# Row sums on TensorE by four f32 matmuls of 32 columns, in a two-layer graph network kernel

## The chip, the cores and the metric

One core of a Trainium2 chip. The metric is the device time of one execution in microseconds (us), the median of several runs.

## The reference

Two graph layers over a dense adjacency matrix of 8192 x 8192 and features of 8192 x 128, all f32, each with a residual and a layer norm:

```python
def _L0_gnn_ref(X, adj, W, b):
    adj_hat = adj + jnp.eye(adj.shape[0], dtype=adj.dtype)
    d_inv_sqrt = 1.0 / jnp.sqrt(jnp.sum(adj_hat, axis=1))
    adj_norm = adj_hat * d_inv_sqrt[:, None] * d_inv_sqrt[None, :]
    out = adj_norm @ (X @ W) + b
    return jax.nn.relu(out)

def _L1_gnn_ref(x, adj, weight, self_weight):
    support = x @ weight
    output = support + adj @ support
    output = output + x @ self_weight
    output = jax.nn.relu(output)
    return pair_norm(output)          # mean of columns taken off, one common scale

x = _layernorm(x + _L0_gnn_ref(x, adj, L0_gnn_W, L0_gnn_b), axis=-1)
x = _layernorm(x + _L1_gnn_ref(x, adj, L1_gnn_weight, L1_gnn_self_weight), axis=-1)
```

The first layer can multiply a column block of adj only when the row sums (degrees) of the same rows are known, since they scale the features.

## The kernel before

adj is cut into 8 x 8 blocks of 1024 x 1024, and each block into four chunks of 1 MiB (128 partitions x 2048). A chunk has two slices of 128 x 1024. The host lays adj out twice, transposed (adjT) and plain (adjN).

**Products.** f32 products are made of f32r parts. For a slice ScalarE writes the rounded value into one of four buffers hi (L558), VectorE writes the rest, raw - hi, as raw_low over the raw chunk itself (L726: `twin` at L321 gives one place in SBUF two names, f32 and f32r), and TensorE does six matmuls of 128 stationary x 512 moving columns (L1043, L1045, L1049) into a pair of PSUM banks. In the trace the low part is raw_low, s_low, zr_low or o_low, after the place in which the chunk lies. Semaphores carry this: `hi_ready`, `slice_split`, `slice_multiplied`. ScalarE may be four slices ahead of TensorE (DEEP = 4).

**Degrees.** In the first phase blocks on and above the diagonal are needed for row sums before their product. Row sums right of the diagonal come from adjN chunks of kind "sum" on ScalarE (L564) or VectorE (L732), the diagonal's from VectorE additions into colsum (chunks "keep", L742, L746). Those of blocks below the diagonal are taken by TensorE while it has them for the product: chunks with `summed`, 112 of them. For each of their slices, `add_sums` multiplies hi and low with a window of `pick`, 128 x 128 and zero but for one column of ones, into pC and pD (L1025). The window's place chooses the PSUM partition in which the sums of this row block collect. `close_sums` (L1061, f32) adds colsum when a row block is complete, ScalarE copies pC and pD into t1 and t2 (L573), and `turn_degree` (L1071) picks partition k out of them with one column of ident, as a column per 128 rows. Then come square root, reciprocal and the scaled features of this row block.

**Order.** One list, `chunks`, sets the order on all engines. The first phase runs over 12 units (a row block's q quarters of 256 rows). In a unit the products of the previous rows stand mixed with the sum chunks of the next. Two more phases follow: both layers' products together, then what is left of the second layer's. SyncE issues the loads in the same order (L486 keep, L493 others), each into the buffer that has been free longest, and waits where that is still in use. The buffers of the first phase are raw0 to raw5 and five borrowed places: s34 and s56 throughout, z67 up to row block 5, z45 up to 3, z23 up to 1. TensorE, ScalarE, VectorE and SyncE each work through their own part strictly in this order.

Of the kernel before, what the change touches and what calls it, by code (L numbers as in the profile page):

```python
# [8 lines left out]
class Chunk:  # L9
# [7 lines left out]
    cached: bool = False  # L17
    act: bool = False
    summed: bool = False
    stage: int = -1  # L20
    tail: int = -1
    buf: str = ""
# [30 lines left out]
def graph_kernel(nc, x, xT, adjT, adjN, W0, b_rows, W1, Wself, out):  # L53
    f32 = mybir.dt.float32
# [5 lines left out]
    P = 128  # L60
# [12 lines left out]
    BG = BLK // P  # L73
    DEEP = 4
    PLACES = 4
    EPS_LN = 1e-5
    EPS_PN = 1e-6
    L0, L1 = 0, 1
# [107 lines left out]
    after_row0 = next(c for c in chunks if c.stage == 1)  # L186


    slices = act_sums = dve_sums = 0
    for chunk in chunks:  # L190
        if chunk.kind == "mul":
            chunk.base = slices
            slices += JB
            chunk.freed = ("multiplied", slices)
            visits[chunk.visit].end = slices
        elif chunk.kind == "sum" and chunk.act:
            act_sums += 1
            chunk.freed = ("act", act_sums)
        elif chunk.kind == "sum":
            dve_sums += 1  # L200
            chunk.freed = ("dve", dve_sums)
# [2 lines left out]

    BORROWED = {"s34": NB - 1, "s56": NB - 1, "z67": 5, "z45": 3, "z23": 1}
    LATE = ("z67", "z45", "z23")
    free_buffers = deque([(f"raw{r}", ()) for r in range(6)] + [(b, ()) for b in BORROWED])
    loads = defaultdict(int)
    phase1_last = {}
    late = False  # L210
    for chunk in chunks:
        if chunk.kind == "keep" or chunk.cached:
            continue
        phase = visits[chunk.visit].phase if chunk.kind == "mul" else 1
        if phase == 3 and not late:
            late = True
            free_buffers.extend((b, ("split", chunk.base)) for b in LATE)
        while phase < 3 and free_buffers[0][0] in BORROWED and (
                phase == 2 or units[chunk.stage][0] > BORROWED[free_buffers[0][0]]):
            free_buffers.popleft()  # L220
        chunk.buf, chunk.after = free_buffers.popleft()
        loads[chunk.buf] += 1
        chunk.load = loads[chunk.buf]
        free_buffers.append((chunk.buf, chunk.freed))
        if phase == 1:
            phase1_last[chunk.buf] = chunk.freed
# [84 lines left out]
    with ctx:  # L311
        def sb(name, shape, dt=f32):
            return ctx.enter_context(nc.sbuf_tensor(name, shape, dt))
# [4 lines left out]
        def sem(name):  # L318
            return ctx.enter_context(nc.semaphore(name))
# [18 lines left out]
        w1 = sb("w1", [P, P])  # L338
        wsum = sb("wsum", [P, P])
        ident = sb("ident", [P, P])  # L340
        rows = sb("rows", [P, P])
        pick = sb("pick", [P, P + NB - 1], f32r)
        d = sb("d", [P, N // P])
# [44 lines left out]
        ident_ready = sem("ident_ready")  # L388
        pick_zero = sem("pick_zero")
        setup = sem("setup")  # L390
        hi_ready = sem("hi_ready")
        slice_split = sem("slice_split")
        slice_multiplied = sem("slice_multiplied")
# [81 lines left out]
        def low_of(chunk, j):  # L475
            if chunk.cached:
                return o1_low[:, chunk.q * TILE + j * BLK:chunk.q * TILE + (j + 1) * BLK]
            return raw_low[chunk.buf][:, j * BLK:(j + 1) * BLK]

        @block.sync  # L480
# [216 lines left out]
        def _(dve):  # L697
# [15 lines left out]
            V.memset(pick[:, NB - 1:NB].bitcast(f32), 1.0).then_inc(setup, 1)  # L713
            dve.wait_ge(consts_in, 64)
            V.tensor_add(wsum[:, :], w1[:, :], t1[:, 0:P]).then_inc(setup, 1)

            def split_lo(chunk):
                for j in range(JB):
# [296 lines left out]
        def _(pe):  # L1015
            T = nc.tensor
            closed = [0]

            def add_sums(chunk, n):

                pe.wait_ge(sums_read, closed[0])
                to = pick[:, NB - 1 - chunk.row:NB - 1 - chunk.row + P]
                for h in range(H):
                    for mov in (hi[n % DEEP][:, :], low_of(chunk, n - chunk.base)):
                        last = T.matmul(sums[h][:, :], to, mov[:, h * HALF:(h + 1) * HALF],  # L1025
                                        start=False, stop=False, skip_group_check=True)
                return last

            def multiply(chunk):
                v = visits[chunk.visit]  # L1030
                for j in range(JB):
                    n = chunk.base + j
                    pe.wait_ge(slice_split, n + 1)
                    end = n == v.end - 1
                    for l, s in zip(chunk.layers, chunk.slots):
                        banks = acc[v.sets[l]]
                        opens = chunk.opens and j == 0
                        for by, count in v.waits[l] if opens else ():
                            pe.wait_ge(bank_free[by], count)
                        a, b = rhi[s][:, j * P:(j + 1) * P], rlo[s][:, j * P:(j + 1) * P]  # L1040
                        for h in range(H):
                            part = slice(h * HALF, (h + 1) * HALF)
                            T.matmul(banks[h][:, :], a, hi[n % DEEP][:, part], start=opens, stop=False,  # L1043
                                     skip_group_check=True)
                            T.matmul(banks[h][:, :], a, low_of(chunk, j)[:, part], start=False, stop=False,  # L1045
                                     skip_group_check=True)
                        for h in range(H):
                            part = slice(h * HALF, (h + 1) * HALF)
                            last = T.matmul(banks[h][:, :], b, hi[n % DEEP][:, part], start=False, stop=end,  # L1049
                                            skip_group_check=True)  # L1050
                        if end and chunk.layers == (L0, L1) and l == L0:
                            last.then_inc(l0_closed, 1)
                    if chunk.summed:
                        last = add_sums(chunk, n)
                    last.then_inc(slice_multiplied, 1)

            def close_sums(k):
                pe.wait_ge(col_step, (k + 1) * (JB * Q - 1))
                to = pick[:, NB - 1 - k:NB - 1 - k + P].bitcast(f32)
                for h in range(H):  # L1060
                    last = T.matmul(sums[h][:, :], to, colsum[:, h * HALF:(h + 1) * HALF],  # L1061
                                    start=(k == 0), stop=True, skip_group_check=True)
                last.then_inc(sums_closed, 1)
                closed[0] = k + 1

            def turn_degree(k):
                pe.wait_ge(sums_read, k + 1)
                if k > 0:
                    pe.wait_ge(z_ready, unit_of[k, 0])
                for g in range(BG):  # L1070
                    last = T.matmul(pA[:, g:g + 1], (t1, t2)[g // G][:, g % G * P:g % G * P + P], ident[:, k:k + 1],  # L1071
                                    start=True, stop=True)
                last.then_inc(deg_turned, 1)

# [52 lines left out]
            pe.wait_ge(consts_in, 64)  # L1127
            pe.wait_ge(setup, 2)
            pe.wait_ge(ident_ready, 1)
            close_sums(0)  # L1130
            turn_degree(0)
            first_product(0)
# [54 lines left out]
```

## Time and profile before

| | us |
|---|---|
| median of 3 runs | 1891.78 |
| lowest, highest | 1887.06, 1892.68 |
| profiled execution | 1891.55 |
| its span | 1889.8 |

The profile shows one execution. Engines: PE is TensorE's matmuls, PEld its weight loads, DVE is VectorE, ACT is ScalarE, SPq is the queue on which SyncE issues loads. A busy share is a mean over the span. Matmuls overlap in their pipeline, so two rows that start 0.23 us apart may each last 0.39 us; the distance of starts is what one costs. L12 is line 12 of the kernel.

### The profile page before, as it was taken

What the parts mean: (1) busy time and instruction counts of PE and PEld (TensorE: products, weight loads), DVE (VectorE), ACT (ScalarE), POOL (GpSimd) and SP (SyncE); (2) the same over time, 40 slices, a digit from 0 to 9 for tenths busy, and PEclk for the clock granted to TensorE, in tenths of its full rate; (3) what the DMA queues carried; (4) which work ended last, traced back from release to release, by engine and by line L of the source; (5) the groups of instructions that cost most, each with busy time, mean ns of one, the idle gap of its engine ahead of it and who ended that gap; (6) DMA issues with size and microseconds to landing.
All of it is one profiled execution on the core that took longest, in us unless ns stands there. A gap on an engine that the chain in (4) does not pass through costs nothing.

```text
span 1889.8 us, 20584 instructions
## 1 busy us (share of the span) xinstructions
PE 1752.6 (93%) x7682; PEld 1418.1 (75%) x7682; DVE 1488.8 (79%) x1985; ACT 1205.6 (64%) x1640; POOL 21.3 (1%) x42
## 2 busy tenths in 40 slices
PE   2879998987999999989999999999989999999993
PEld 1657886865887888767788888888868888877872
DVE  4889788767878789986777575575589999999997
ACT  4576685784757556654554554455468888888875
POOL 0000000000000000100000000000000000000001
PEclk7899999998999999999999999999999999999995
DMA  9999999899898686954544445555589999999943
GB/s 398 421 421 421 417 400 422 337 392 394 348 402 345 234 356 244 358 197 148 174 163 189 167 175 197 182 178 189 191 304 385 385 388 386 386 379 366 386 193 89
DMA packets 87459, 572.03 MB, mean 303 GB/s; under 512 B 8960, under 2 KB 17152, under 8 KB 19264
## 3 DMA queue, kind: packets, MB, share of 16 engines
q1 hardware_dynamic: 84928, 562.07, 75.8%
q0 software_dynamic: 2432, 8.65, 1.4%
q8 instruction: 60, 0.98, 0.2%
q14 instruction: 39, 0.32, 0.0%
HBM read 566.49 MB, written 4.19 MB: 302 GB/s over the span
## 4 chain that ended last, share of the span: by engine, by line
PE 74%; DVE 14%; DMA 6%; ACT 4%; issue 2%; SPq 0%; ACTq 0%; DVEq 0%
PE acc L1043 18%; PE acc L1045 18%; PE acc L1049 18%; DMA raw<-in_adjT 4%; PE pC L1025 4%; PE pD L1025 4%; DVE raw_low L726 4%; DMA s<-in_adjN 2%; ACT hi L558 2%; DVE o_low L726 1%; DVE s L732 1%; DVE zr_low L726 1%; DVE ux L805 1%; PE pA L1043 1%; PE pB L1045 1%
## 5 line engine op out<-in xcount | busy, mean ns | idle before, releaser
L1043 PE MATMUL acc<-hi,rhi 128*128 128x512 f32 x1792 | 726.3, 405 | 76.3 <-DVE raw_low L726 25.0
L726 DVE TENSOR_TENSOR raw_low<-raw,hi 128x1024 fp32r<-128x1024 f32 x576 | 684.3, 1220 | 84.4 <-ACT hi L558 79.8
L558 ACT ACTIVATE hi<-raw 128x1024 fp32r<-128x1024 f32 x576 | 593.7, 1055 | 195.3 <-DMA raw<-in_adjT 68.3
L1049 PE MATMUL acc<-hi,rlo 128*128 128x512 f32 x1792 | 559.9, 394 | 0.0
L1045 PE MATMUL acc<-raw_low,rhi 128*128 128x512 f32 x1348 | 530.7, 394 | 0.0
L1043 PEld LDWEIGHTS acc<-hi,rhi 128*128 128x128 f32 x1792 | 341.7, 191 | 173.4 <-DVE raw_low L726 35.0
L1049 PEld LDWEIGHTS acc<-hi,rlo 128*128 128x128 f32 x1792 | 341.2, 190 | 73.7
L1045 PEld LDWEIGHTS acc<-raw_low,rhi 128*128 128x128 f32 x1348 | 256.2, 190 | 54.9 <-issue 3.6
L726 DVE TENSOR_TENSOR zr_low<-zr,hi 128x1024 fp32r<-128x1024 f32 x148 | 177.6, 1221 | 30.4 <-ACT hi L558 27.9
L558 ACT ACTIVATE hi<-zr 128x1024 fp32r<-128x1024 f32 x148 | 155.2, 1059 | 58.4 <-PE pD L1025 24.0
L725 DVE TENSOR_TENSOR rlo<-zr,rhi 128x256 fp32r<-128x256 f32 x123 | 52.0, 423 | 177.5 <-ACT hi L558 177.5
L552 ACT ACTIVATE rhi<-zr 128x256 fp32r<-128x256 f32 x123 | 50.8, 413 | 191.7 <-PE acc L1049 190.3
L564 ACT ACTIVATE raw<-raw 128x1024 f32<-128x1024 f32 x98 | 102.3, 1046 | 23.7 <-DMA raw<-in_adjN 23.7
L1025 PE MATMUL pC<-hi,pick 128*128 128x512 f32 x224 | 89.8, 401 | 0.0
L1025 PE MATMUL pD<-hi,pick 128*128 128x512 f32 x224 | 89.0, 397 | 0.0
L1045 PE MATMUL acc<-zr_low,rhi 128*128 128x512 f32 x212 | 83.7, 395 | 0.0
L558 ACT ACTIVATE hi<-s 128x1024 fp32r<-128x1024 f32 x52 | 54.4, 1058 | 45.6 <-PE pD L1025 34.1
L805 DVE TENSOR_TENSOR ux<-ux,acc 128x512 f32<-128x512 f32 x122 | 77.9, 679 | 0.0
L726 DVE TENSOR_TENSOR o_low<-o,hi 128x1024 fp32r<-128x1024 f32 x64 | 75.7, 1217 | 2.7 <-ACT hi L558 2.7
L726 DVE TENSOR_TENSOR s_low<-s,hi 128x1024 fp32r<-128x1024 f32 x52 | 62.1, 1220 | 19.4 <-ACT hi L558 19.2
L558 ACT ACTIVATE hi<-o 128x1024 fp32r<-128x1024 f32 x64 | 66.6, 1055 | 16.3 <-PE pD L1025 12.7
L725 DVE TENSOR_TENSOR rlo<-s,rhi 128x256 fp32r<-128x256 f32 x148 | 62.0, 419 | 9.1 <-ACT hi L558 8.5
(187 smaller groups left out, 1813.9 us busy)
## 6 DMA issues: line engine op xcount, KB each, us to landing
raw<-in_adjT SPq DMA_DIRECT2D x288, 1024.0 KB, 5.1
zr<-in_adjT SPq DMA_DIRECT2D x74, 1024.0 KB, 5.4
raw<-in_adjN SPq DMA_DIRECT2D x67, 1024.0 KB, 13.8
o<-in_adjT SPq DMA_DIRECT2D x32, 1024.0 KB, 11.0
s<-in_adjT SPq DMA_DIRECT2D x26, 1024.0 KB, 16.6
zr<-in_adjN SPq DMA_DIRECT2D x23, 1024.0 KB, 11.7
s<-in_adjN SPq DMA_DIRECT2D x22, 1024.0 KB, 12.4
s<-in_xT POOLq DMA_DIRECT2D x8, 512.0 KB, 7.0
```

What stands on the lines that cost most here:

```text
L552: S.activation(rhi[s][:, :], src[:, at:at + JB * P], ACT.Copy)
L558: S.activation(hi[n % DEEP][:, :], slice_of(chunk, j), ACT.Copy).then_inc(hi_ready, 1)
L564: ins = S.activation(slice_of(chunk, j), slice_of(chunk, j), ACT.Copy, accum_out=rsum[chunk.row % 2][:, g:g + 1])
L725: V.tensor_sub(rlo[s][:, :], (zr, s1)[l][:, at:at + JB * P], rhi[s][:, :].bitcast(f32))
L726: V.tensor_sub(low_of(chunk, j), slice_of(chunk, j), hi[n % DEEP][:, :].bitcast(f32)).then_inc(slice_split, 1)
L732: V.tensor_reduce(rsum[chunk.row % 2][:, g:g + JB], raw[chunk.buf].rearrange("p (g j) -> p g j", g=JB), AX.X, ALU.add).then_inc(dve_summed, 1)
L805: ins = V.tensor_copy(u, a) if v.first else V.tensor_add(u, u, a)
L1025: last = T.matmul(sums[h][:, :], to, mov[:, h * HALF:(h + 1) * HALF], start=False, stop=False, skip_group_check=True)
L1043: T.matmul(banks[h][:, :], a, hi[n % DEEP][:, part], start=opens, stop=False, skip_group_check=True)
L1045: T.matmul(banks[h][:, :], a, low_of(chunk, j)[:, part], start=False, stop=False, skip_group_check=True)
L1049: last = T.matmul(banks[h][:, :], b, hi[n % DEEP][:, part], start=False, stop=end, skip_group_check=True)
```

## The change

Row sums are no longer taken from the split parts of each slice but from the raw f32 chunk, ahead of its product. Four f32 matmuls do a chunk: two slices times two halves of 512 columns. The stationary operand is a window of pick with 32 columns, and each matmul writes its own quarter of PSUM partitions, 0 to 31, 32 to 63 and so on, in turn in pC, pD, pC, pD. The sums of a row block thus lie in four partitions 32 apart, and `turn_degree` adds them up with a column of the new tensor quarters, which has a one in each of the four. Since the raw chunk must stay whole until TensorE has summed it, low parts of summed chunks are no longer written over it, but into four slots of 128 x 1024 in raw4 and raw5. These two leave the pool of load buffers until the second phase.

```diff
+    LOWS = 2 * JB
+            if chunk.summed:
+                chunk.low = summed % LOWS
+                summed += JB
+                last_summed = slices
...
-    free_buffers = deque([(f"raw{r}", ()) for r in range(6)] + [(b, ()) for b in BORROWED])
+    free_buffers = deque([(f"raw{r}", ()) for r in range(4)] + [(b, ()) for b in BORROWED])
...
+        if phase == 2 and not own:
+            own = True
+            free_buffers.extend((b, ("multiplied", last_summed)) for b in FOR_LOWS)
...
+            if chunk.summed:
+                at = (chunk.low + j) % JB * BLK
+                return raw_low[FOR_LOWS[(chunk.low + j) // JB]][:, at:at + BLK]
...
+            V.tensor_add(quarters[:, :], ident[:, 0:NB], ident[:, QUARTER:QUARTER + NB]).then_inc(quarters_step, 1)
+            for t in (2, 3):
+                dve.wait_ge(quarters_step, t - 1)
+                V.tensor_add(quarters[:, :], quarters[:, :],
+                             ident[:, t * QUARTER:t * QUARTER + NB]).then_inc(quarters_step, 1)
...
-            def add_sums(chunk, n):
+            def add_sums(chunk):
+                pe.wait_ge(*landed(chunk))
                 pe.wait_ge(sums_read, closed[0])
-                to = pick[:, NB - 1 - chunk.row:NB - 1 - chunk.row + P]
-                for h in range(H):
-                    for mov in (hi[n % DEEP][:, :], low_of(chunk, n - chunk.base)):
-                        last = T.matmul(sums[h][:, :], to, mov[:, h * HALF:(h + 1) * HALF],
-                                        start=False, stop=False, skip_group_check=True)
-                return last
+                to = pick[:, NB - 1 - chunk.row:NB - 1 - chunk.row + QUARTER].bitcast(f32)
+                for t in range(JB * H):
+                    j, h = t // H, t % H
+                    T.matmul(sums[h][t * QUARTER:(t + 1) * QUARTER, :], to,
+                             slice_of(chunk, j)[:, h * HALF:(h + 1) * HALF], start=False, stop=False,
+                             skip_group_check=True)
...
             def multiply(chunk):
                 v = visits[chunk.visit]
+                if chunk.summed:
+                    add_sums(chunk)
...
-                    if chunk.summed:
-                        last = add_sums(chunk, n)
                     last.then_inc(slice_multiplied, 1)
...
-                    last = T.matmul(pA[:, g:g + 1], (t1, t2)[g // G][:, g % G * P:g % G * P + P], ident[:, k:k + 1],
+                    last = T.matmul(pA[:, g:g + 1], (t1, t2)[g // G][:, g % G * P:g % G * P + P], quarters[:, k:k + 1],
```

On TensorE, the first summed chunk, before (acc is the product's pair of banks, x2 two matmuls in a row):

```order
L1043 MATMUL acc<-hi,rhi 128x512 [waits slice_split]
L1045 MATMUL acc<-raw_low,rhi 128x512
L1043 MATMUL acc<-hi,rhi 128x512
L1045 MATMUL acc<-raw_low,rhi 128x512
L1049 MATMUL acc<-hi,rlo 128x512 x2
L1025 MATMUL pC<-hi,pick 128x512 [waits sums_read]
L1025 MATMUL pC<-raw_low,pick 128x512
L1025 MATMUL pD<-hi,pick 128x512
L1025 MATMUL pD<-raw_low,pick 128x512
L1043 MATMUL acc<-hi,rhi 128x512 [waits slice_split]
```

The same place in the change (L1051 is the new add_sums; 32x512 is stationary columns x moving columns):

```order
L1051 MATMUL pC<-raw,pick 32x512 [waits sums_read,loaded_raw2]
L1051 MATMUL pD<-raw,pick 32x512
L1051 MATMUL pC<-raw,pick 32x512
L1051 MATMUL pD<-raw,pick 32x512
L1071 MATMUL acc<-hi,rhi 128x512 [waits slice_split]
L1073 MATMUL acc<-raw_low,rhi 128x512
L1071 MATMUL acc<-hi,rhi 128x512
L1073 MATMUL acc<-raw_low,rhi 128x512
L1077 MATMUL acc<-hi,rlo 128x512 x2
L1071 MATMUL acc<-hi,rhi 128x512 [waits slice_split]
```

Four matmuls for each slice behind its product have become four for the chunk ahead of it, and they wait for the load instead of the split.

SyncE's queue at the start, before (o is the place of the kept chunks; s and zr are the borrowed ones):

```order
L493 DMA raw<-in_adjN 128x2048 x6
L493 DMA s<-in_adjN 128x2048 x2
L493 DMA zr<-in_adjN 128x2048 x3
L493 DMA raw<-in_adjT 128x2048 [waits act_summed]
```

and in the change:

```order
L510 DMA raw<-in_adjN 128x2048 x4
L510 DMA s<-in_adjN 128x2048 x2
L510 DMA zr<-in_adjN 128x2048 x3
L510 DMA raw<-in_adjN 128x2048 [waits act_summed] x2
```

Behind the four kept chunks, the first load that has to wait for a buffer is the tenth instead of the twelfth; the order of the loads themselves is the same.

## Rows read from the trace of the kernel before

**Rows 1.** The page's busy times: engine, us, share of the span, instructions.
```profile
PE 1752.6 (93%) x7682; PEld 1418.1 (75%) x7682; DVE 1488.8 (79%) x1985; ACT 1205.6 (64%) x1640; POOL 21.3 (1%) x42
```

**Rows 2.** The page's 40 slices: TensorE's granted clock and the DMA engines, in tenths.
```profile
PEclk7899999998999999999999999999999999999995
DMA  9999999899898686954544445555589999999943
```

**Rows 3.** Stretches: from:to, length, busy us (records) by engine, clock, DMA share, GB/s.
```profile
49.00:188.70 139.70, 118.76 (x466) 92.70 (x465) 124.66 (x131) 85.41 (x119) 0.00 (x0) 0.92 1.01 421
188.70:323.50 134.80, 130.05 (x566) 104.84 (x565) 109.12 (x118) 92.83 (x129) 0.53 (x1) 0.97 1.00 413
323.50:459.00 135.50, 117.92 (x483) 93.19 (x482) 97.31 (x106) 92.55 (x137) 0.53 (x1) 0.92 0.92 372
459.00:551.00 92.00, 91.25 (x409) 73.68 (x407) 73.88 (x79) 63.03 (x84) 0.53 (x1) 1.00 0.94 384
551.00:626.00 75.00, 72.43 (x327) 58.22 (x326) 59.18 (x64) 48.17 (x63) 0.53 (x1) 1.00 0.89 360
626.00:697.00 71.00, 71.00 (x326) 58.14 (x324) 56.03 (x63) 41.94 (x51) 0.53 (x1) 1.00 0.68 270
697.00:757.00 60.00, 59.86 (x279) 49.53 (x278) 50.14 (x58) 34.10 (x38) 0.53 (x1) 1.00 0.64 262
```

**Rows 4.** Waits: us, times, longest; PE in 459:757, SPq in 459:757, PE in 49:459.
```profile
PE acc L1043 <- DVE o_low L726: 2.5, 2, 1.8
PE acc L1043 <- DVE raw_low L726: 0.7, 1, 0.7
...
SPq L493 <- PE pD L1025: 180.2, 41, 9.9
...
PE acc L1043 <- DVE raw_low L726: 14.0, 6, 5.1
PE acc L1043 <- DVE zr_low L726: 6.4, 2, 3.6
PE acc L1043 <- DVE o_low L726: 3.3, 2, 2.8
PE acc L1043 <- DVE s_low L726: 1.2, 2, 0.8
```

**Rows 5.** Timeline of TensorE: start us, duration; two slices of a summed chunk.
```profile
574.75 0.39 PE L1025 MATMUL pC<-hi,pick 128*128 128x512 f32 x1
...
577.02 0.39 PE L1025 MATMUL pC<-hi,pick 128*128 128x512 f32 x1
```

**Rows 6.** Stretches again, the instructions of L1025 alone.
```profile
49.00:188.70 139.70, 47.23 (x168) 33.18 (x168) 0.92 1.01 421
188.70:323.50 134.80, 52.75 (x192) 36.53 (x192) 0.97 1.00 413
323.50:459.00 135.50, 45.29 (x160) 31.50 (x160) 0.92 0.92 372
459.00:551.00 92.00, 34.70 (x128) 23.95 (x128) 1.00 0.94 384
551.00:626.00 75.00, 26.08 (x96) 17.94 (x96) 1.00 0.89 360
...
697.00:757.00 60.00, 15.05 (x56) 10.44 (x56) 1.00 0.64 262
```

**Rows 7.** L1061: its weight loads (ns min/median/max), and one row opening in the timeline.
```profile
L1061 PEld LDWEIGHTS pC<-s,pick x16: 187/188/333, 19.4 to 757.5; 128*128 128x128 f32 x16
...
549.59 1.02 PE L1061 MATMUL pC<-s,pick 128*128 128x512 f32 x2
550.45 1.02 PE L1061 MATMUL pD<-s,pick 128*128 128x512 f32 x2
```

**Rows 8.** The page's groups of splits: count, busy us, mean ns, idle time before.
```profile
L726 DVE TENSOR_TENSOR raw_low<-raw,hi 128x1024 fp32r<-128x1024 f32 x576 | 684.3, 1220 | 84.4 <-ACT hi L558 79.8
L558 ACT ACTIVATE hi<-raw 128x1024 fp32r<-128x1024 f32 x576 | 593.7, 1055 | 195.3 <-DMA raw<-in_adjT 68.3
```

More of the change, by code:

```diff
@@ L19 @@
     summed: bool = False
+    low: int = -1
     stage: int = -1
@@ L75, in graph_kernel @@
     PLACES = 4
+    QUARTER = P // 4
     EPS_LN = 1e-5
@@ L186, in graph_kernel @@
     after_row0 = next(c for c in chunks if c.stage == 1)
-    slices = act_sums = dve_sums = 0
+    LOWS = 2 * JB
+    slices = act_sums = dve_sums = summed = 0
     for chunk in chunks:
@@ L206, in graph_kernel @@
     LATE = ("z67", "z45", "z23")
-    free_buffers = deque([(f"raw{r}", ()) for r in range(6)] + [(b, ()) for b in BORROWED])
+    FOR_LOWS = ("raw4", "raw5")
+    free_buffers = deque([(f"raw{r}", ()) for r in range(4)] + [(b, ()) for b in BORROWED])
+    own = False
     loads = defaultdict(int)
@@ L340, in graph_kernel @@
         ident = sb("ident", [P, P])
+        quarters = sb("quarters", [P, NB])
         rows = sb("rows", [P, P])
@@ L390, in graph_kernel @@
         setup = sem("setup")
+        quarters_step = sem("quarters_step")
         hi_ready = sem("hi_ready")
@@ L715, in _ @@
             V.tensor_add(wsum[:, :], w1[:, :], t1[:, 0:P]).then_inc(setup, 1)
+            dve.wait_ge(ident_ready, 1)
+            V.tensor_add(quarters[:, :], ident[:, 0:NB], ident[:, QUARTER:QUARTER + NB]).then_inc(quarters_step, 1)
[3 more added lines that the diff above has]
+                             ident[:, t * QUARTER:t * QUARTER + NB]).then_inc(quarters_step, 1)
             def split_lo(chunk):
@@ L1129, in _ @@
             pe.wait_ge(ident_ready, 1)
+            pe.wait_ge(quarters_step, 3)
             close_sums(0)
```

## The prediction

> **What bounds the kernel now.** I read the busy shares first, then the slices, then the stretch that the change touches, cut at the row openings of L1061.
>
> [rows 1]: the span is 1889.8 us, TensorE is busy for 93% of it, VectorE 79%, ScalarE 64%. [rows 2]: in the first 15 or so of the 40 slices the DMA engines are at 9 tenths with few gaps, and TensorE's granted clock is often below full there. So the first phase has two candidates for its limit, and the averages hide which. Every row-sum matmul (L1025) lies in this first phase, before 757 us.
>
> [rows 3] settles it by stretch. In 49 to 188.7 us the DMA share is 1.01 at 421 GB/s and TensorE leaves time over. In 188.7 to 323.5 both are nearly full. In 323.5 to 459 the transfers have a share of 0.92. From 459 to 757 us TensorE is busy for practically all of 298 us at a clock of 1.00, while the DMA rate falls to 262 to 384 GB/s. [rows 4] agrees: between 459 and 757 us the matmuls wait 3.2 us in all, and the DMA queue waits 180.2 us for the L1025 matmul that frees its buffer. TensorE time added or removed behind 459 us moves the end nearly one to one; before it, it is partly hidden.
>
> What a matmul costs in a stream is the distance of starts, not its duration. [rows 5]: L1025 starts at 574.75, and ten matmuls later (six of a slice's product, four of its sums) the next slice's starts at 577.02. That is 2.27 us, or 0.227 us for each. A summed chunk (two slices) takes 4.54 us, of which its eight sum matmuls are 1.82 us.
>
> To know what is left over in each stretch I set its records at full speed (records of [rows 3] times 0.227 us, less some 3 us for each row opening in it, whose 32 small matmuls take about half as long as they are charged) against its length:
> - 49 to 188.7: 466 x 0.227 = 106 us of 139.7; 34 us left over. DMA needs all of it.
> - 188.7 to 323.5: 128 - 3 = 125 of 134.8; 9 us left. DMA at 421 GB/s needs 134.8 x 413/421 = 132 us.
> - 323.5 to 459: 110 - 3 = 107 of 135.5; 29 us left. DMA needs 135.5 x 372/421 = 120 us.
> - 459 to 757: 1341 records, 304 less about 12 = 292 of 298 us; 6 us left. DMA needs 92 x 384/421 = 84, then 64, 46 and 37 us.
>
> The sum matmuls of these stretches are 168, 192, 160 and 376 records ([rows 6]); at eight for a chunk these are 21, 24, 20 and 47 of the 112 summed chunks.
>
> **The change, part by part.**
>
> *Removed:* eight matmuls of 0.227 us for each summed chunk, 1.82 us, or 204 us over 112.
>
> *Added:* four f32 matmuls with a stationary operand of 32 columns. [rows 7] has an f32 matmul of the same 512 moving columns, though with 128 stationary columns: L1061 writes pC and then pD, and each shows two records. The first one starts at 549.59, the second at 550.45, so an f32 matmul takes 0.86 us, two records of 0.43 us. Four in a row cost 3.44 us; all four side by side, on four separate quarters of the columns, cost 0.86 us. These are the bounds from the rows, and the sign of the result lies between them, with break-even at 1.82 us. No row shows a matmul on a quarter of the array, nor two at once.
>
> I take a value between them, by this argument: the rows show matmuls starting strictly in the order of the program, and an f32 matmul is two records with a weight load ahead of each (x16 loads beside x16 matmuls for eight matmuls into pC, [rows 7]). The second record of tile 0 needs the columns that its first one holds, so it starts 0.43 us later; the first record of tile 1 comes behind it in order, and can run beside it, and so on. That is a staircase: the first record alone, three pairs, the last record alone: 5 x 0.43 = 2.15 us. Around it the array changes from products over all columns to quarters and back. A product lasts 0.39 us at a spacing of 0.227 ([rows 5]); if the pipeline has to empty at both changes, that is 2 x 0.16 = 0.32 us, and nothing if not. I take 0.25, nearer to emptying, since the last tile's columns are needed by the next product. Sum: 2.4 us for a chunk, 0.58 us more than before.
>
> The Trainium skill, in the page "TensorE: Matmul & The Clock Gate", section "Part 3: Packing small matmuls — row/col tiling", says that matmuls at different column tiles run at the same time, with starts some 4 ns apart; by that alone the four would end after about one f32 matmul. No row here shows it; that reading is the first rival below. The page "TensorEngine Tiling (Array Packing)", section "Key Properties", says that a change of tiling mode drains the engine, which speaks against the change; the 0.32 us worked out above would be its whole price for a chunk.
>
> *Moved:* the sums stand ahead of the chunk's product and wait for the landed raw chunk alone, where they stood behind each slice's product and its split. They can fill the time that ScalarE (1.06 us for a slice) and VectorE (1.22 us) take to split ([rows 8]). It helps only where TensorE waits for a split: 24.9 us in 49 to 459 us are products that wait for low parts ([rows 4], its four rows of that stretch), and there the transfers set the pace anyway. I take 2 us of gain; bounds 0 and 10. The wait has little behind it to hurt: if the chunk has not landed, its product could not run either.
>
> *Buffers:* raw4 and raw5 leave the pool of the first phase, which falls from 11, 10, 9 and 8 buffers to 9, 8, 7 and 6 as the borrowed ones run out. With transfers of 1 MiB at 421 GB/s (2.5 us each) six buffers go round in 15 us in the DMA-bound case; a chunk holds one for its landing (about 5 us) and about 7 us of splitting and multiplying. It is enough, closely. Where DMA is short of work (share 0.64 to 0.94) TensorE sets the pace and refills come in time. Nothing for the likely case; bounds 0 and 10 us. Low parts in their own four slots wait for no one new: hi already allows VectorE four slices of lead.
>
> *Small:* turning the degrees uses a column with four ones instead of one, at the same size; three short additions at the start. Nothing.
>
> **The sum**, on the profiled execution, whose own time is 1891.55 us, beside a median of 1891.78:
> - 459 to 757: 47 chunks x 0.58 = 27 us, 1 of it into what is left over: +26.
> - 188.7 to 323.5: 24 x 0.58 = 14 us against 9 left over: 125 + 14 = 139 us against 134.8; with some waits remaining, +7.
> - 323.5 to 459: 20 x 0.58 = 12; 107 + 12 = 119 us is about what DMA needs: +2.
> - 49 to 188.7: 21 x 0.58 = 12 into 34 us left over: 0.
> - earlier start of the sums: -2.
> Together +33 us: 1925 us.
>
> **The rivals.**
>
> *Full overlap (faster).* All four tiles run at the same time, or the two records of each do not hold up the next: 0.86 + 0.25 = 1.1 us, 0.7 us less than before. Behind 459 us that is 47 x 0.7 = 33 us, of which the transfers (84 and 64 us of 92 and 75) leave 30; before it they leave some 3 and 7 us. Total -40: 1852 us. For it: separate columns, separate PSUM partitions. Against it: the in-order pairs of records.
>
> *No overlap (slower by much).* The quarters run one after another: 3.44 + 0.25 = 3.7 us, +1.9 for a chunk. 47 x 1.9 - 4 = +85; 125 + 46 = 171 against 134.8, +36; 107 + 38 = 145, +9; the first stretch 106 + 40 = 146, +6. Total +136: 2028 us. For it: all matmul records of the trace follow each other at their full spacing. Between it and my forecast lies a staircase whose weight loads can't be fetched ahead: four loads of up to 0.19 us (the 188 ns of [rows 7]), 3.1 us for a chunk, some +80.
>
> *Even.* The overlap ends near 1.8 us, for instance by a staircase whose ends mesh with the products; the time stays within a few us of 1892.
>
> *The other side by another way:* with full overlap and too few buffers, transfers would pace the phase; it turns from -40 to no gain only if each of the four stretches loses 10 us, which is the upper bound above. I count it in the even case.
>
> **How the numbers follow.** Staircase 0.48 (own range 1905 to 1960), full overlap 0.28 (1838 to 1870), no overlap or nearly none 0.16 (1985 to 2050), even 0.08. The range 1843 to 1980 leaves out the case of no overlap and a little of the fast side. Faster by over 0.3% (about the least that a measurement of this kernel can tell from none) 0.29, within it 0.07, slower 0.64.
>
> **What would show it.** In the changed kernel's timeline: from the first quarter matmul to the first product behind it, 2.4 us by the staircase, 1.1 by full overlap, 3.7 by none; the records of two tiles overlapping in pairs. In the stretches: the four row openings behind 459 us further apart by 16, 12, 12 and 7 times the difference for a chunk. The DMA queue should still wait mostly for TensorE. What is behind 757 us should keep its length. The prediction is wrong if tiles start together, if none overlap, or if TensorE sits idle for data where it was full.

## The result

The changed kernel takes 1871.26 us (median of 4 runs, 1867.84 to 1878.05) beside 1890.65 us for the kernel before: ratio 0.9904, 95% interval 0.9889 to 0.9919, so 1.0% faster. I had forecast 1925 us. The sign was wrong. Medians and ratios below are of fast runs; one slow execution of `before_half`, at 4774.95 us, is left out.

The profiled execution has a span of 1866.0 us, 23.8 us shorter than before. The page of the changed kernel (engine, busy us, share, instructions; then the slices of the granted clock and of DMA, which answer to [rows 1, 2]):

```profile
PE 1683.6 (90%) x7682; PEld 1263.3 (68%) x7682; DVE 1487.0 (80%) x1988; ACT 1203.6 (65%) x1640; POOL 21.2 (1%) x42
...
PEclk7889999988999999999999999999999999999995
DMA  9999999999999678844444455545589999999943
```

The DMA engines now show 9 tenths in each of the first 13 slices, where [rows 2] had three dips to 8 among them. The same cut by row opening as in [rows 3] (length, busy us and records of each engine, clock, DMA share, GB/s):

```profile
49.00:186.40 137.40, 103.99 (x464) 63.35 (x464) 122.22 (x129) 85.15 (x119) 0.00 (x0) 0.91 1.01 421
186.40:315.30 128.90, 116.50 (x566) 72.78 (x565) 110.29 (x121) 92.38 (x129) 0.53 (x1) 0.95 1.01 418
315.30:449.00 133.70, 106.82 (x485) 65.60 (x484) 96.30 (x106) 93.51 (x137) 0.53 (x1) 0.90 0.95 390
449.00:536.50 87.50, 80.43 (x405) 50.83 (x404) 72.20 (x77) 61.18 (x84) 0.53 (x1) 1.00 0.95 387
536.50:606.80 70.30, 64.07 (x326) 41.60 (x325) 58.40 (x64) 47.78 (x64) 0.53 (x1) 1.00 0.96 394
606.80:673.30 66.50, 64.00 (x326) 41.56 (x325) 55.92 (x63) 41.79 (x52) 0.53 (x1) 1.00 0.75 301
673.30:735.00 61.70, 58.43 (x286) 41.12 (x285) 53.92 (x63) 35.94 (x40) 0.53 (x1) 1.00 0.71 282
```

TensorE is no longer full behind the third opening (80.4 of 87.5 us), while the DMA share is 0.95 there. The openings themselves, by the start of close_sums in the timelines:

| row block opened | 1 | 2 | 3 | 4 | 5 | 6 | 7 |
|---|---|---|---|---|---|---|---|
| before, us | 187.8 | 322.41 | 458.76 | 549.59 | 624.13 | 695.43 | 757.55 |
| changed, us | 185.6 | 314.43 | 448.20 | 535.68 | 605.91 | 672.42 | 733.78 |
| saved since the last | 2.2 | 5.8 | 2.6 | 3.4 | 4.3 | 4.8 | 0.8 |

Everything saved lies in the first phase. What is behind it keeps its length, 1132 us from the last opening to the end in both. In stretches of 1085 us there, set 23.6 us apart, TensorE is busy for 1061.92 us in one and 1061.70 us in the other.

Now the sums themselves, in the timeline of TensorE (start, duration; L1077 ends the product before, L1051 is the new `add_sums`, L1071 begins the next product):

```profile
561.50 0.62 PE L1077 MATMUL acc<-hi,rlo 128*128 128x512 f32 x2
562.05 0.62 PE L1051 MATMUL pC<-zr,pick 128*32 128x512 f32 x1
562.05 0.62 PE L1051 MATMUL pD<-zr,pick 128*32 128x512 f32 x1
562.06 0.62 PE L1051 MATMUL pC<-zr,pick 128*32 128x512 f32 x1
562.07 0.62 PE L1051 MATMUL pD<-zr,pick 128*32 128x512 f32 x1
562.50 0.59 PE L1051 MATMUL pC<-zr,pick 128*32 128x512 f32 x1
562.51 0.59 PE L1051 MATMUL pD<-zr,pick 128*32 128x512 f32 x1
562.51 0.59 PE L1051 MATMUL pC<-zr,pick 128*32 128x512 f32 x1
562.52 0.59 PE L1051 MATMUL pD<-zr,pick 128*32 128x512 f32 x1
563.04 0.50 PE L1071 MATMUL acc<-hi,rhi 128*128 128x512 f32 x1
...
565.99 0.62 PE L1051 MATMUL pC<-raw,pick 128*32 128x512 f32 x1
```

All four first records start within 20 ns, and 0.45 us later all four second ones. There is no staircase. From one chunk's sums to the next is 565.99 - 562.05 = 3.94 us, against 4.54 before ([rows 5], two slices). The twelve product matmuls are 2.73 of it at the 0.227 us of [rows 5], so the sums cost 1.2 us and save 0.6 for a chunk: 0.86 for the two rows of records and 0.35 around them. Over 112 chunks that is 67 us of TensorE time. The stretches say the same: TensorE is busy for 594.3 us from 49 to 735 us, and was for 661.3 from 49 to 757. The question is where the other 43 us went (48 by the medians, which differ by 19).

The waits of TensorE show what became of them (us in total, times, longest). `ux` is the sum into which VectorE reads the product's PSUM banks, so TensorE waits there for banks to be read; `t` is ScalarE's copy of pC and pD. The changed kernel from 49 to 735 us:

```profile
PE acc L1071 <- DVE ux L829: 27.6, 10, 7.2
PE acc L1071 <- DVE raw_low L750: 24.1, 26, 2.3
PE pC L1051 <- DMA raw<-in_adjT: 11.3, 4, 4.6
PE acc L1071 <- DVE o_low L750: 8.5, 8, 2.6
PE pC L1051 <- ACT t L590: 7.6, 6, 1.3
PE pC L1051 <- DMA s<-in_adjT: 6.9, 3, 4.2
PE pC L1051 <- DMA zr<-in_adjT: 5.6, 3, 3.2
```

They sum to 91.6 us. In the kernel before, from 49 to 757 us, this view gives 46.4 us:

```profile
PE acc L1043 <- DVE ux L805: 18.3, 10, 5.4
PE acc L1043 <- DVE raw_low L726: 14.8, 7, 5.1
PE acc L1043 <- DVE zr_low L726: 6.4, 2, 3.6
PE acc L1043 <- DVE o_low L726: 5.7, 4, 2.8
PE acc L1043 <- DVE s_low L726: 1.2, 2, 0.8
```

So 67 us less work less 45 us more waiting leaves 22, near the 23.8 measured. Of the 45 us, 24 are landings of the raw chunk, for which the sums now wait themselves, 9 the banks that VectorE reads, 8 the copy of pC and pD, and 5 low parts. ScalarE, from which the low parts come, waits with its hi 107.9 us for landings in this phase, against 80.2 before.

One more thing changed that no run here separates. In the first three stretches the granted clock is 0.91, 0.95 and 0.90, and in [rows 3] it was 0.92, 0.97 and 0.92. Stretch by stretch, the length times what the clock lacks to 1.00 gives 32 us for the changed kernel and 26 for the one before, so by this estimate some 6 us of TensorE's full speed went there, inside its busy time.

The experiments ask who makes TensorE wait. All ratios are against the kernel before.

### The profile page after: what moved, and what is told of

It reads as the page before. It is cut to its first block, busy times and chain, and to the rows that moved or that the text cites. A ratio compares the mean times of both kernels' runs of the same rounds, so it can differ in the third digit from the quotient of the medians.

```text
span 1866.0 us, 20699 instructions
## 1 busy us (share of the span) xinstructions
PE 1683.6 (90%) x7682; PEld 1263.3 (68%) x7682; DVE 1487.0 (80%) x1988; ACT 1203.6 (65%) x1640; POOL 21.2 (1%) x42
## 4 chain that ended last, share of the span: by engine, by line
PE 66%; DVE 18%; DMA 9%; ACT 3%; issue 2%; SPq 1%; ACTq 0%; DVEq 0%
PE acc L1071 18%; PE acc L1073 17%; PE acc L1077 17%; DVE raw_low L750 6%; PE pC L1051 3%; DMA raw<-in_adjT 3%; DVE o_low L750 2%; DMA s<-in_adjT 2%; DMA zr<-in_adjT 2%; DVE s L770 2%; DMA zr<-in_adjN 1%; ACT hi L575 1%; DVE ux L829 1%; DVE s L756 1%; PE pA L1071 1%
## 5 line engine op out<-in xcount | busy, mean ns | idle before, releaser
L1071 PE MATMUL acc<-hi,rhi 128*128 128x512 f32 x1792 | 735.6, 411 | 90.2 <-DVE raw_low L750 34.4
L750 DVE TENSOR_TENSOR raw_low<-raw,hi 128x1024 fp32r<-128x1024 f32 x552 | 654.8, 1220 | 55.7 <-ACT hi L575 50.5
L575 ACT ACTIVATE hi<-raw 128x1024 fp32r<-128x1024 f32 x552 | 567.3, 1054 | 166.2 <-PE acc L1077 80.5
L1073 PE MATMUL acc<-raw_low,rhi 128*128 128x512 f32 x1520 | 601.9, 396 | 0.0
L1077 PE MATMUL acc<-hi,rlo 128*128 128x512 f32 x1792 | 561.8, 395 | 0.0
L1071 PEld LDWEIGHTS acc<-hi,rhi 128*128 128x128 f32 x1792 | 342.8, 191 | 273.8 <-DVE raw_low L750 91.6
L1077 PEld LDWEIGHTS acc<-hi,rlo 128*128 128x128 f32 x1792 | 342.6, 191 | 75.2
L1073 PEld LDWEIGHTS acc<-raw_low,rhi 128*128 128x128 f32 x1520 | 291.1, 192 | 59.4 <-issue 3.3
L750 DVE TENSOR_TENSOR zr_low<-zr,hi 128x1024 fp32r<-128x1024 f32 x108 | 129.8, 1222 | 7.7 <-ACT hi L575 5.2
L581 ACT ACTIVATE raw<-raw 128x1024 f32<-128x1024 f32 x80 | 83.6, 1047 | 37.4 <-DMA raw<-in_adjN 37.4
L750 DVE TENSOR_TENSOR raw_low<-s,hi 128x1024 fp32r<-128x1024 f32 x60 | 71.1, 1220 | 30.0 <-ACT hi L575 29.4
L1051 PE MATMUL pC<-raw,pick 128*32 128x512 f32 x228 | 62.1, 620 | 15.1 <-DMA raw<-in_adjT 11.3
L750 DVE TENSOR_TENSOR raw_low<-zr,hi 128x1024 fp32r<-128x1024 f32 x50 | 59.0, 1220 | 18.4 <-ACT hi L575 18.2
L1051 PE MATMUL pD<-raw,pick 128*32 128x512 f32 x228 | 62.1, 621 | 0.0
```

The source lines that it names most:

```text
L575: S.activation(hi[n % DEEP][:, :], slice_of(chunk, j), ACT.Copy).then_inc(hi_ready, 1)
L581: ins = S.activation(slice_of(chunk, j), slice_of(chunk, j), ACT.Copy, accum_out=rsum[chunk.row % 2][:, g:g + 1])
L750: V.tensor_sub(low_of(chunk, j), slice_of(chunk, j), hi[n % DEEP][:, :].bitcast(f32)).then_inc(slice_split, 1)
L1051: T.matmul(sums[h][t * QUARTER:(t + 1) * QUARTER, :], to, slice_of(chunk, j)[:, h * HALF:(h + 1) * HALF], start=False, stop=False, skip_gr ...
```

## Is it the separate columns?

`same_quarter` lets all four matmuls write the same quarter:

```diff
-                    T.matmul(sums[h][t * QUARTER:(t + 1) * QUARTER, :], to,
+                    T.matmul(sums[h][0:QUARTER, :], to,
```

> The changed kernel, but all four f32 matmuls of a chunk write PSUM partitions 0 to 31, so that all use the same 32 columns of the array; same instructions, same operands. Theory: it is the separate columns that let the four run at once (1.08 us for a chunk in the changed kernel). Then they run in a row here: 4 x 0.86 + 0.25 = 3.7 us, and the time is that of my case of no overlap, about 2028 us (1985 to 2050). Rival: 32 stationary columns are cheap by themselves, wherever they lie: the time stays near the 1871 us of the changed kernel.

2066.7 us, ratio 1.0934 (1.0919 to 1.0949). Its timeline:

```profile
700.75 1.05 PE L1051 MATMUL pC<-zr,pick 128*32 128x512 f32 x2
701.63 1.02 PE L1051 MATMUL pD<-zr,pick 128*32 128x512 f32 x2
702.49 1.02 PE L1051 MATMUL pC<-zr,pick 128*32 128x512 f32 x2
703.35 1.02 PE L1051 MATMUL pD<-zr,pick 128*32 128x512 f32 x2
704.30 0.50 PE L1071 MATMUL acc<-hi,rhi 128*128 128x512 f32 x1
```

Starts are 0.86 us apart, and 3.55 us pass from the first to the next product, against 0.99 in the change. The columns are what matters; 32 columns alone are not cheaper than 128. The time is 39 us above my 2028 and nearly 1% above the range given. The 0.10 us more around each group explains 11 of the 39. TensorE is busy here for 860.3 of the 884 us from 49 to 933, so I had also let too much of the added work vanish in what was left over.

`order_0011` asks about the order of starts, the ground of my staircase. Two quarters get two matmuls each:

```diff
-                for t in range(JB * H):
+                for t in (0, 2, 1, 3):
                     j, h = t // H, t % H
-                    T.matmul(sums[h][t * QUARTER:(t + 1) * QUARTER, :], to,
+                    T.matmul(sums[h][h * QUARTER:(h + 1) * QUARTER, :], to,
```

> The changed kernel with two quarters instead of four: the four matmuls write quarters 0, 0, 1, 1 in this order. Each quarter has two matmuls of 0.86 us to do, 1.72 us. If matmuls may start only in program order, the third starts with the second and ends after it: 3 x 0.86 = 2.6 us and 0.3 around it, 2.9 us for a chunk. If each quarter takes its matmuls as they come: 1.72 + 0.3 = 2.0 us.

1915.11 us (1.0139, 1.0124 to 1.0155). Its timeline, one chunk:

```profile
500.07 0.62 PE L1051 MATMUL pC<-raw,pick 128*32 128x512 f32 x1
500.09 0.62 PE L1051 MATMUL pD<-raw,pick 128*32 128x512 f32 x1
...
501.39 0.59 PE L1051 MATMUL pC<-raw,pick 128*32 128x512 f32 x1
501.40 0.59 PE L1051 MATMUL pD<-raw,pick 128*32 128x512 f32 x1
```

The program asks for pC, pC, pD, pD. Yet pD's first record starts 20 ns after pC's first, not behind pC's fourth, and the pairs stay together to the end; from the first to the next product 1.85 us pass, 0.86 more than in the change. Here each quarter worked through its own matmuls, without waiting for another's that stands ahead in the program. The profile gives start times only, so whether the engine itself changed the order or something ahead of it did is not shown.

## Is it the smaller pool?

`before_pool` is the kernel before with four own buffers in the first phase:

```diff
-    free_buffers = deque([(f"raw{r}", ()) for r in range(6)] + [(b, ()) for b in BORROWED])
+    free_buffers = deque([(f"raw{r}", ()) for r in range(4)] + [(b, ()) for b in BORROWED])
...
+        if phase == 2 and not own:
+            own = True
+            free_buffers.extend((b, ("multiplied", last_summed)) for b in ("raw4", "raw5"))
```

> The kernel before, with raw4 and raw5 taken out of the pool until the second phase, as in the change; nothing else. The changed kernel gained 19 us where full overlap should have given some 40. Theory V (VectorE has become the bound where kept chunks are added up): the pool costs nothing much here, 0 to 3 us. Theory B (the smaller pool lets TensorE run out of data and took the rest of the gain): 12 to 20 us slower than before, about 1906.

1901.88 us (1.0062, 1.0049 to 1.0074): 12 us slower. Its windows show where (compare [rows 3]):

```profile
188.70:323.50 134.80, 128.41 (x563) 103.37 (x562) 108.78 (x118) 92.25 (x128) 0.53 (x1) 0.99 0.98 394
323.50:459.00 135.50, 112.50 (x466) 88.79 (x464) 91.61 (x101) 90.34 (x133) 0.53 (x1) 0.94 0.91 365
459.00:551.00 92.00, 88.81 (x389) 71.22 (x390) 70.70 (x77) 59.75 (x82) 0.53 (x1) 0.98 0.91 364
```

Transfers fall from 413 to 394, 372 to 365 and 384 to 364 GB/s: with fewer buffers a load waits longer for one to come free, and the time is not made up later. TensorE's busy time in the phase is the same as before (660.5 and 661.3 us), and its waits rise from 46.4 to 57.2 us, which is nearly all of the 12.

`after_pool8` takes one more buffer (raw3) out of the changed kernel's pool, the same edit with `range(3)`.

> The changed kernel with one more buffer, raw3, taken out of the pool until the second phase (8 to 5 buffers). Theory B: the pool is short already, so one less costs another 6 to 12 us, 1877 to 1884. Rival (the transfers' rate alone is the limit, not when they can start): about 1871.

1888.02 us (0.9997, 0.9988 to 1.0006): 17 us above the changed kernel, its whole gain. The rate in 449 to 536.5 us is 351 GB/s instead of 387. The first phase gets 24 us longer in the profile (last opening at 757.9 instead of 733.8 us), and only half of that is waiting: to the last opening TensorE waits 103.8 instead of 91.6 us and is busy for 605.8 instead of 594.3 us. In 449 to 606.8 us its granted clock is 0.92, where the changed kernel has 1.00. The expectation of 6 to 12 us held the waits and not this.

`low3` goes the other way. Low parts get three slots, two in raw5 and one in an idle stretch of s1, and raw4 returns to the pool:

```diff
-    LOWS = 2 * JB
+    LOWS = 3
...
+                slot = (chunk.low + j) % LOWS
+                if slot == 2:
+                    return s1_low[:, 7 * BLK:8 * BLK]
+                return raw_low["raw5"][:, slot * BLK:(slot + 1) * BLK]
...
+                    if chunk.summed and chunk.low + j >= LOWS:
+                        dve.wait_ge(slice_multiplied, summed_slices[chunk.low + j - LOWS] + 1)
```

> The changed kernel with low parts in three slots instead of four: two in raw5 and one in an idle stretch of s1, so that raw4 goes back to the pool (10, 9, 8 and 7 buffers instead of 9, 8, 7 and 6); VectorE waits in addition until the summed slice three back is multiplied. Theory B (each buffer out of the pool costs: 12 us for two in the kernel before, 17 us for one more in the changed kernel): 5 to 10 us less than the changed kernel, 1861 to 1866. Rival (the changed kernel sits at the transfers' rate already, and only a still smaller pool hurts): 1869 to 1873.

1866.5 us (0.9877, 0.9864 to 0.9891), 5 us below the changed kernel and the fastest here that does all of the work. It lies between the two expectations, and its interval just touches that of the changed kernel (0.9889 to 0.9919), so this step alone proves little. Its direction fits the other two, which are clear: the pool was a price, and I had set it at nothing.

`ahead_inplace` tried to have all buffers and the quarters. Low parts stay over the raw chunk, and TensorE sums a chunk between the two slices of the product ahead:

```diff
+                    if chunk.summed and j == 0:
+                        dve.wait_ge(raw_summed, summed_at[id(chunk)])
...
+                    if j == 1 and after is not None and after.summed:
+                        add_sums(after)
```

> Quarter sums with the whole pool of load buffers: low parts are written over the raw chunk as in the kernel before, and TensorE does the four f32 matmuls of a chunk between the two slices of the product chunk ahead of it, so that VectorE may overwrite it in time. Theory B (the pool of 9 to 6 buffers took 12 us or so of the change's gain, since loads come too late): 1855 to 1862 us. Rival (loads are late because the transfers themselves are near their limit, or TensorE now waits in the middle of a chunk for the landing of the next): no better than the changed kernel, 1868 us or more.

1891.58 us (1.0012, 1.0003 to 1.0021): all of the gain is lost. VectorE has a new wait, here from 49 to 449 us:

```profile
DVE raw_low L740 <- PE pD L1040: 37.6, 24, 4.4
DVE s_low L740 <- PE pD L1040: 14.3, 7, 4.5
DVE zr_low L740 <- PE pD L1040: 14.2, 10, 3.1
```

That is 66 us in which the split stands still for the sums, a wait that the change's separate slots avoid. It reaches TensorE only in part. Up to its last opening at 756 us TensorE waits 95.0 us, 3 more than in the changed kernel, but it is busy for 612.8 us instead of 594.3, at the same mean clock of 0.95. So the greater part of the loss is busy time, for the same matmuls in other places; what makes it longer is not shown. The run does not tell what the full pool would be worth.

## Is it VectorE, or the place of the sums?

`before_nocol` and `after_nocol` leave out six of the seven additions into colsum for each row block:

```diff
-                    return
-                for j in range(JB):
-                    dve.wait_ge(col_step, k * (JB * Q - 1) + q * JB + j - 1)
-                    V.tensor_add(colsum, colsum, slice_of(chunk, j)).then_inc(col_step, 1)
...
-                pe.wait_ge(col_step, (k + 1) * (JB * Q - 1))
+                pe.wait_ge(col_step, k + 1)
```

> The kernel before without six of the seven additions into colsum for each row block on VectorE (the diagonal's share of the row sums is left out). Takes 7.2 us of VectorE work from each of eight row blocks. Theory V: TensorE was the bound there before, so it gains little, 0 to 6 us. Theory B: says nothing about VectorE; 0 to 6 us as well.

> The changed kernel without six of the seven additions into colsum for each row block (the same part left out). Theory V: VectorE's 4.67 us for a product chunk beside two additions (two splits 2.3, two additions 2.4) holds TensorE, which needs 3.85; without them it gains 10 to 15 us on the changed kernel, about 1858, and the distance to the kernel before without them widens from 19 to 28 us or more. Theory B: the gain is no larger than in the kernel before, and the distance stays near 19 us.

1882.5 us (0.9961, 0.9948 to 0.9973) and 1866.71 us (0.9879, 0.9864 to 0.9894): 7 us gained before the change, 5 after, distance 16. The theory of VectorE falls. It had come from a place in the changed kernel's timeline (590 to 603 us) where chunks come every 4.67 us, two splits and two additions; the run shows that such places cost little here. With the loads eased, further down, the additions weigh a little more.

`kept_pe` sums the diagonal blocks of rows 1 to 7 by quarters on TensorE and spares VectorE the additions:

```diff
...
             def close_sums(k):
+                if k > 0:
+                    sum_kept(k).then_inc(sums_closed, 1)
+                    closed[0] = k + 1
+                    return
```

> The changed kernel with the diagonal blocks (kept chunks) of row blocks 1 to 7 also summed by quarter matmuls: at each row opening TensorE does 16 f32 matmuls in four sets (4 x 0.86 = 3.4 us) instead of the two of close_sums (1.7 us), and VectorE is spared seven additions of 1.2 us. Theory: without six of these additions the changed kernel gained 4.6 us; TensorE's 1.9 us more at each of seven openings cost up to 13 us, so 1871 to 1880. Rival (VectorE holds more than that run showed): 1860 to 1867.

1878.89 us (0.995, 0.9937 to 0.9964), 8 us above the changed kernel, as the first theory had it. VectorE is busy for 58 us less up to the last opening, TensorE for 16 us more, and TensorE's waits fall by 9 us only: its time is the dearer one.

`sums_mid` puts the sums between a chunk's slices:

```diff
-                if chunk.summed:
-                    add_sums(chunk)
                 for j in range(JB):
                     n = chunk.base + j
+                    if chunk.summed and j == 1:
+                        add_sums(chunk)
```

> The changed kernel with the sums of a chunk between its two slices instead of ahead of the first. After a row opening the first slice then covers ScalarE's copy of pC and pD, for which TensorE waits 1.27 us at each of seven openings in the changed kernel. If these waits are on the path: 6 to 9 us less, about 1863. If what follows an opening waits for data anyway: about 1871.

1874.34 us (0.9925, 0.9913 to 0.9938): not 8 us faster, and the median is 3 us slower, though the two intervals overlap. The waits for ScalarE's copy and for landings ahead of the sums are gone (2.5 and 23.4 us in 49 to 449 us), and the one for low parts rises from 14.7 to 38.7 us:

```profile
PE acc L1071 <- DVE raw_low L750: 38.7, 18, 4.2
```

So most of it is the same lateness of the loads, now met behind the split. All waits together fall, from 91.6 to 82.4 us up to the last opening. What grows is TensorE's busy time, to 609.2 us from 594.3, with the same mean clock of 0.95, as in `ahead_inplace`. Both put the sums between two slices; why that makes TensorE's busy time longer is not shown.

## Is it the transfers?

`before_half` and `after_half` load and sum only half of each chunk of kind sum:

```diff
+                    if chunk.kind == "sum":
+                        sp.dma_start(raw[chunk.buf].rearrange("p (j f) -> p j f", j=JB)[:, :, 0:HALF],
...
-                    ins = S.activation(slice_of(chunk, j), slice_of(chunk, j), ACT.Copy,
+                    ins = S.activation(slice_of(chunk, j)[:, 0:HALF], slice_of(chunk, j)[:, 0:HALF], ACT.Copy,
```

> The kernel before with only half of each chunk of kind sum loaded (first 512 columns of each slice) and summed on ScalarE and VectorE; the rest is left out. That takes 14% of the first phase's transfers away with some work on both engines, and nothing from TensorE. TensorE's own work is the limit of much of the phase before the change, so the gain is small: 25 to 45 us, about 1855 us.

> The changed kernel with the same half of the sum chunks left out. A summed chunk takes TensorE 3.95 us instead of 4.54, 0.6 us less, 67 us over 112 chunks, of which the change kept 19. If the rest went to transfers (and what hangs on them), it comes back here: the distance to the kernel before with the same half left out is 50 to 67 us. Rival: it went to waits that have nothing to do with loads (the copy of pC and pD at openings, order of the sums); then the distance stays at 20 to 30 us.

1858.17 us (0.9824, 0.9804 to 0.9843) and 1823.26 us (0.9638, 0.9623 to 0.9653). The kernel before gains 33 us, the changed one 48, and the distance grows from 19 to 35 us. That lies between the two expectations: halving the sum chunks gives back 16 of the 48 missing us, not all.

The waits of the phase agree. To its end (691 and 729 us) TensorE waits 61.1 us in the changed kernel and 32.1 in the one before, 29 more instead of 45, and its direct waits for landings fall from 23.8 to 4.2 us. One rival stays: ScalarE sums half as much here, and from 49 us to the end of the phase it is busy for 399 us instead of 458, while VectorE's time hardly changes. The runs do not separate the loads from this relief.

The last two runs leave out both, half of each sum chunk and the additions into colsum.

> The kernel before with half of each sum chunk and six of seven colsum additions per row block left out. TensorE's work is the limit of the phase here; so a little less than the 1860 us with the sum chunks halved: 1850 to 1857.

> The changed kernel with the same two parts left out. If VectorE's additions hold TensorE once the loads are eased: 15 to 25 us below the 1823 us of the halved sum chunks alone, about 1803, and 45 to 55 us from the kernel before with the same parts left out. If not: 1815 to 1820, and the distance stays at 35 to 40 us.

1850.47 us (0.979, 0.9776 to 0.9805) and 1810.29 us (0.9583, 0.9567 to 0.9599): distance 40. With the loads eased, VectorE's additions are worth 13 us in the changed kernel and 8 in the kernel before, so they widen the distance by 5 us only. What is left shows in the changed kernel's waits from 40 to 730 us (67.4 us in all, 37.7 in the kernel before with the same parts left out):

```profile
PE acc L1072 <- DVE ux L830: 19.4, 10, 3.9
PE acc L1072 <- DVE o_low L755: 17.3, 7, 9.1
PE acc L1072 <- DVE raw_low L755: 15.0, 12, 2.6
PE pC L1052 <- ACT t L595: 7.6, 6, 1.3
PE pC L1052 <- DMA raw<-in_adjT: 7.1, 2, 5.4
```

7.6 of the 30 us more are the copy at openings, 8 a landing that TensorE now waits for itself. Ahead of VectorE stands ScalarE, and from 40 to 690 us its hi waits for landings for 80 us here and 31 there:

```profile
ACT hi L580 <- DMA raw<-in_adjT: 46.8, 23, 5.2
ACT hi L580 <- DMA s<-in_adjT: 20.6, 10, 4.7
ACT hi L580 <- DMA zr<-in_adjT: 12.5, 8, 4.0
```

So even with half the sum loads gone, loads come late. With nine to six buffers that fits the pool, but no run here has the eased loads with the full pool; how the last 27 us divide between pool, copy, clock and the order of the loads stays open.

## Why the prediction was wrong

**What bounds the kernel** held for the kernel before: the phase in two halves, the cost of a summed chunk (4.54 us), the stretches, the unchanged length behind 757 us. "TensorE time added or removed behind 459 us moves the end nearly one to one" did not hold for time removed: TensorE's busy time there fell by 27.6 us, and the four stretches got 13.2 us shorter.

**Added, the step that failed:** "the first record of tile 1 comes behind it in order, and can run beside it, and so on. That is a staircase". I took 2.4 us for a chunk; it is 1.2, so each of the 112 chunks saves 0.6 us where I had it cost 0.58 more. The two records of an f32 matmul hold up only their own quarter. I had made a rule of order out of rows that held only full-width matmuls; `same_quarter` shows that matmuls on the same columns run in a row anyway, so such rows say nothing on the order of separate ones. The sentence of the Trainium skill that I set beside it ("TensorE: Matmul & The Clock Gate", "Part 3: Packing small matmuls — row/col tiling": tiles run at once, starts some 4 ns apart) agrees with the trace, where the four first records start within 20 ns. I had read it as silent on pairs of records and given the rival 0.28; with the sign hanging on this alone, an argument without a row did not deserve the higher chance.

**The change around the group:** taken as 0.25 us, measured 0.35. The Trainium skill's page "TensorEngine Tiling (Array Packing)", "Key Properties", has the engine drain at a change of mode; the gap fits, and it is 0.03 above my upper bound from [rows 5].

**Full overlap,** the rival that came true, was put at 1852 us; the measured 1871 lies outside the 1838 to 1870 I gave it, narrowly. Its saving for a chunk was 0.7 and is 0.6. Its 30 us behind 459 us became 13, and its 10 before it became 11. I had let the DMA engines reach 421 GB/s there and counted no waits. From 449 to 606.8 us the changed kernel moved 387 and 394 GB/s, at a share of 0.95 and 0.96. TensorE waits in all four stretches, 19 us against 3 before: for low parts whose split came late, and 5 us for ScalarE's copy.

**Buffers:** "Nothing for the likely case; bounds 0 and 10 us" was the second failed step. Two buffers cost 12 us in the kernel before. I had argued from a mean round of 15 us for six buffers; the loads are queued in a fixed order, with kept loads that wait for their own place (80.9 us behind 459 us before the change). That what counts is how far the queue gets ahead of such a stop is my reading; no run tests it.

**Moved:** 2 us of gain, bounds 0 and 10. No run has the new sums behind the product, so this stays untested; `sums_mid`, with the middle of the chunk, differs by 3 us only. What I missed is the 1.27 us wait for ScalarE's copy at six openings.

The range, 1843 to 1980, held the time because it reached over to the rival. That is luck: the forecast in it was wrong in sign, and the time was reached by an overlap I had at 0.28 and a price of buffers I had at nothing.

## What to carry to other kernels

Where f32 matmuls have 32 stationary columns or fewer, give each its own 32 and its own PSUM quarter: four of them cost here what one does, plus about 0.35 us for going to quarters and back, so do all of a chunk's in one group. Count the buffers that such a rewrite ties up before counting its gain: near balance of transfers and TensorE, two load buffers cost 12 us before the change and one more cost all of the 19 us after it. And when TensorE is relieved in a phase where the DMA share is already above 0.9, expect much of the gain to turn into waits: here 45 of 67 us did.

## What the runs showed of the hardware

- f32 matmuls on different column quarters run side by side, both records of each; the two rows of records take about 0.86 us, like one matmul of 128 columns ([rows 7]), and 0.99 us pass to the next product. On one and the same quarter it is 3.55 us (`same_quarter`).
- In the trace each quarter takes its matmuls in turn without waiting for another's that stand ahead in the program (`order_0011`, quarters 0, 0, 1, 1: 1.85 us to the next product; starts in the order of the program would give 2.7 by an estimate, three times 0.86 and 0.13 behind).
- A weight load of 32 columns is recorded with 109 ns against 188 for 128:

```profile
L1051 PEld LDWEIGHTS pC<-raw,pick x228: 106/109/153, 51.3 to 725.0; 128*32 128x32 f32 x114
```
